# Edge attention in a four-block network: the whole mask on VectorE, finished rows normalised by GpSimd, weighted turned rows written by ScalarE

## The reference, cut to what matters

```python
def edge_score(a):
    s = jnp.einsum('bid,bjd->bij', hidden * a, hidden)
    return jax.nn.leaky_relu(s, 0.2)
alpha = jnp.where(adj == 1, edge_score(a0), NEG_INF)   # a1..a3 for adj == 2, 3, 4
alpha = jax.nn.softmax(alpha, axis=-1)
return jnp.matmul(alpha, hidden)      # x = x + this, hidden = layernorm(x)
```

## Time and profile before

| | us |
|---|---|
| median of 3 runs (lowest, highest) | 1168.76 (1166.08, 1174.06) |
| the profiled execution, its own time | 1170.39 |
| its span, first to last instruction | 1168.6 |
| TensorE busy in it | 1100.7 (94%) |
| VectorE, ScalarE, GpSimd busy in it | 704.9, 744.0, 415.9 |
| edge attention: 64 steps, from first to last L2031 | 301.7 |

### The profile page before, as it was taken

One profiled execution on the slowest core, in us unless ns is written; L12 is line 12 of the kernel. 1 busy time (PEld: TensorE's weight loads), 2 busy tenths in 40 slices (PEclk: granted clock), 3 DMA queues, 4 the chain that ended last, 5 costly groups with the idle time before them and its releaser, 6 DMA issues. The chain is left out here.

```text
span 1168.6 us, 18925 instructions
## 1 busy us (share of the span) xinstructions
PE 1100.7 (94%) x5993; PEld 725.8 (62%) x5993; DVE 704.9 (60%) x2210; ACT 744.0 (64%) x1074; POOL 415.9 (36%) x475
## 2 busy tenths in 40 slices
PE   2998899899999999689999999998999999999998
PEld 2554445444477777557777777776546666666667
DVE  4779888888663436287888888864443333333335
ACT  2887777788665554366777777775666556565561
POOL 5327677866765222344556565211000000000000
PEclk9999899899999999899999999999999999999999
DMA  8977557655227665412222222110000000000001
GB/s 260 343 292 265 183 214 285 254 207 210 75 89 245 186 195 168 131 44 84 84 82 82 80 84 80 56 54 1 1 1 10 19 10 10 19 10 19 10 10 37
DMA packets 69142, 131.08 MB, mean 112 GB/s; under 512 B 9918, under 2 KB 30764, under 8 KB 68012
## 3 DMA queue, kind: packets, MB, share of 16 engines
q1 hardware_dynamic: 60268, 111.96, 28.5%
q0 software_dynamic: 8192, 16.79, 4.7%
q10 hardware_dynamic: 576, 1.05, 0.3%
HBM read 77.60 MB, written 52.17 MB: 111 GB/s over the span
## 5 line engine op out<-in xcount | busy, mean ns | idle before, releaser
L2227 PEld LDWEIGHTS eY<-Vo,dGW 128*128 128x128 f32 x1024 | 132.4, 191 | 54.0 <-issue 52.8
L507 POOL DMA_INDIRECT sorted_x<-V,AT_I x128 | 125.9, 984 | 55.8 <-issue 36.2
L2210 PE MATMUL eU<-XTN,V 128*128 128x512 f32 x256 | 132.9, 602 | 2.5 <-PEq L2145 2.5
L2227 PE MATMUL eY<-Vo,dGW 128*128 128x128 f32 x1024 | 134.2, 276 | 0.1
L673 PE MATMUL O<-Y,HS 128*128 128x512 f32 x256 | 134.0, 644 | 0.0
L1863 POOL DMA_INDIRECT W<-sorted_y,ROW_I x96 | 101.0, 1052 | 90.5 <-PE f_T L1923 71.7
L2218 PE MATMUL eU<-H,V 128*128 128x512 f32 x256 | 131.4, 595 | 0.0
L2397 DVE TENSOR_TENSOR dGW<-H,WBC 128x512 f32<-128x512 f32 x80 | 55.2, 691 | 125.2 <-PE eY L2227 125.0
L1942 PEld LDWEIGHTS f_O<-f_XN,f_PT 128*128 128x128 f32 x896 | 107.8, 192 | 25.3 <-issue 20.7
L2306 ACT ACTIVATE H<-eU,bn 128x512 f32<-128x512 f32 x128 | 99.5, 777 | 30.4 <-PE eU L2210 21.3
L1995 ACT COPY f_PT<-f_TP 128x512 f32<-128x512 f32 x128 | 68.7, 589 | 73.2 <-PE f_TP L1932 73.2
(11 more groups left out here) (305 smaller groups left out, 2034.2 us busy)
## 6 DMA issues: line engine op xcount, KB each, us to landing
XTN<-in_adj SPq DMA_DIRECT2D x64, 512.0 KB, 4.7
masks<-NMW SPq DMA_DIRECT2D x8, 2048.0 KB
f_MK<-masks SPq DMA_DIRECT2D x60, 256.0 KB, 2.7
sorted_y<-zero SPq DMA_DIRECT2D x39, 256.0 KB, 10.1
NMW<-sorted_x SPq DMA_DIRECT2D x39, 256.0 KB, 2.7
sorted_y<-NMW SPq DMA_DIRECT2D x39, 256.0 KB, 2.5
X<-in_x SPq DMA_DIRECT2D x8, 512.0 KB, 7.7
out_x<-X SPq DMA_DIRECT2D x16, 256.0 KB, 2.3
```

Source lines behind the costliest of these rows:

```text
L507: g_.indirect_dma_start(sorted_x, bass.IndirectOffsetOnAxis(ap=AT_I[b % 2][:, kt:kt + 1], axis=0), XR[b % 2][:, t * P:(t + 1) * P], None). ...
L2210: pe.matmul(U1[j % 2][:, :], V1[:, e * P:(e + 1) * P], XTN[:, b * N + q * HALF:b * N + (q + 1) * HALF], start=True, stop=True).then_inc(u1 ...
L2227: i = pe.matmul(Y[q][:, t * P:(t + 1) * P], GW[:, j % 2, t * P:(t + 1) * P], Vo[:, e * P:(e + 1) * P], start=(e == 0 and t == 0), stop=(e ...
```

## The change

Three pieces of work move to another engine, and one to another form. VectorE adds the mask to all 1024 columns of `R4`; TensorE's identity matmul with the mask, and its wait for the mask load, go. GpSimd does `norm_next`, straight after `root_next` in r = 4, with the negated means in the new tile `LESS`. ScalarE writes `XTA` from `M` with the scale `a0`, just ahead of its copy of `M` into `XT`, and `weigh` goes from VectorE. In r = 0 of a batch TensorE also waits until the second half of `XT` is copied.

```diff
+                def norm_next(b):                        # GpSimd
+                    if b >= 1:
+                        pool.wait_ge(m_ps, nth["n", b - 1, 1] + 1)
+                    nc.gpsimd.tensor_scalar(LESS[:, :], MVN[:, b % 2, :, 0], -1.0, 0.0, ALU.mult, ALU.add).then_inc(pstep, 1)
+                    pool.wait_ge(pstep, step.next())
+                    pool.wait_ge(next_rs_ready, b + 1)
+                    for t in range(NT):
+                        i = nc.gpsimd.tensor_scalar(XNN[:, t * P:(t + 1) * P], X[:, (b * NT + t) * P:(b * NT + t + 1) * P],
+                                                    LESS[:, t:t + 1], RSN[:, 1, t:t + 1], ALU.add, ALU.mult)
+                    i.then_inc(next_xn_ready, 1)
...
                         if r == 4 and b > 0:
                             root_next(b - 1)
+                            norm_next(b - 1)
...
                     if r == 0 and b >= 1:                # TensorE, scores(g)
                         pe.wait_ge(xta_ready, 2 * b)
+                        pe.wait_ge(m_read, nth["x", b, 1] + 1)
                     if g >= 2:
                         pe.wait_ge(y_ready, g - 1)
-                    pe.matmul(T[g % 2][:, 0:HALF], xta(b)[:, r * P:(r + 1) * P], xt(b)[:, 0:HALF], start=True, stop=False)
-                    if g == 0:
-                        pe.wait_ge(late_loaded, 16 * E // 2 * (len(late_loads) + 1))
-                    if g >= RING:
-                        pe.wait_ge(loaded[g % RING], 16 * (g // RING))
-                    pe.matmul(T[g % 2][:, 0:HALF], identb[:, :], mask(g)[:, 0:HALF], start=False, stop=True)
-                    pe.matmul(T[g % 2][:, HALF:N], xta(b)[:, r * P:(r + 1) * P], xt(b)[:, HALF:N], start=True, stop=True
-                              ).then_inc(t_ready, 1)
+                    for h in range(2):
+                        i = pe.matmul(T[g % 2][:, h * HALF:(h + 1) * HALF], xta(b)[:, r * P:(r + 1) * P],
+                                      xt(b)[:, h * HALF:(h + 1) * HALF], start=True, stop=True)
+                    i.then_inc(t_ready, 1)
...
                         if b >= 3:                       # ScalarE, copy_turned, kind "x"
                             act.wait_ge(t_ready, (b - 1) * NT)
-                            act.wait_ge(xta_ready, 2 * b - 4)
+                        nc.scalar.activation(XTA[:, b % 2, h * HALF:(h + 1) * HALF], M[:, :], ACT.Copy, scale=a0
+                                             ).then_inc(xta_ready, 1)
                     nc.scalar.copy(dst, M[:, :]).then_inc(m_read, 1)
...
-                    v.tensor_tensor(R4[:, g % 2, HALF:N], R4[:, g % 2, HALF:N], mask(g)[:, HALF:N], ALU.add).then_inc(barred, 1)
+                    v.tensor_tensor(R4[:, g % 2, :], R4[:, g % 2, :], mask(g), ALU.add).then_inc(barred, 1)
...
-                def norm_next(b):                        # VectorE
-                def weigh(b):                            # VectorE
```

More of the change, by code:

```diff
@@ L1786, in one_kind @@
             STN, MVN, RSN = tile("STN", [P, NT, 6]), tile("MVN", [P, 2, NT, 2]), tile("RSN", [P, 2, NT])
+            LESS = tile("LESS", [P, NT])
             YG = [w[:, :].rearrange("p (k d) -> p k d", d=P) for w in (W1, W2)]
@@ L2052, in mean_next @@
                         i.then_inc(next_mv_ready, 1)
-                def norm_next(b):
-                    if b >= 1:
-                        dve.wait_ge(m_ps, nth["n", b - 1, 1] + 1)
-                    ln_apply(dve, b, MVN[:, b % 2, :, :], RSN[:, 1, :], XNN, 0, next_rs_ready, next_xn_ready)
                 def join(b, tiles):
@@ L2093, in norm @@
                     i.then_inc(xn_ready, 1)
-                def weigh(b):
[L2096 to L2101, removed]
                 joins, joined_at = Count(), {}
@@ L2111, in prepare @@
                             norm(1)
-                        if r == 7:
-                            weigh(1)
                     elif b < LAST:
@@ L2119, in prepare @@
                             norm(b + 1)
-                        if r == 6:
-                            weigh(b + 1)
                     if b + 2 < B and r == 7:
@@ L2133, in _ @@
                     prepare(g // NT, g % NT)
-                    if g >= NT and g % NT == (6 if g < LAST * NT else 5):
-                        norm_next(g // NT - 1)
                 for g in range(G - 3, G):
```

## The result

| | before | after |
|---|---|---|
| median of 20 runs, us | 1171.85 | 1176.79 |
| the profiled execution, its own time / span | 1170.39 / 1168.6 | 1177.56 / 1175.8 |
| first to last reduction, us | 301.73 | 308.27 |

The ratio is 1.0046, with a 95% interval from 1.0024 to 1.0067: half a per cent slower. Of the 7.2 us by which the profiled span grew, 6.5 lie in the 64 steps of the stage. The first reduction starts 1.2 us later and 0.6 us less follows behind the last.

The account below looks back on a forecast made before the run. TensorE, at 4.60 us a plain step, led a circle of 4.25; lengthened to 4.78, the circle would bind. 301.1 + 2.7 + 2.9 + 1.7, less 0.7, against 301.7: 6.0 us slower, about 1174.8 us, range 1163 to 1188.

Parts of the forecast that it names:

- 63 steps at the circle's 4.78: All intervals from first to last reduction, each at the lengthened lap: 301.1 us, against 301.7 before.
- the circle: Closed lap of ScalarE and VectorE: rectifier, mask addition, reduction, exp, next rectifier; 4.25 us before, 4.78 with 0.53 added.
- seven steps with `norm`, +0.39 each: One step per batch where VectorE still normalises before its reduction stays 0.39 us above the circle: 2.7 us.
- steps with `feature`: GpSimd's sum of features holds up VectorE's joins: 0.5 us in three steps, 1.35 in batch 6, together 2.9 us.
- mask additions held off by `norm_next`: VectorE's mask additions wait for one of GpSimd's eight normalisations at most: 0.25 us a batch, 1.7 us in all.
- first tile and first laps: First tile's scores ready earlier without the mask matmul, first laps of batch 0 slightly under 4.25: 0.7 us off.
- the lower of the two bounds: VectorE's mask addition on 1024 columns: 1.22 us, like the reduction, against at most 1.38, two of the present instruction.
- The rival that TensorE stays the bound: Stage stays bound by TensorE, the circle has unseen slack, and 13.4 us come out: 1155 us; chance 0.05.
- ScalarE's second write: Writing `XTA` from `M`, about 0.6 us, two per batch: just fits before the exp, costed at nothing; uncovered, 4 us.
- The upper bound: In r = 5 or 6, each collision of normalisations and mask addition costs up to a whole GpSimd instruction: 0.61 twice a batch.
- the second rival: GpSimd's eight normalisations hold off a mask addition for their whole run, up to 4.3 us a batch: about 1204; chance 0.07.
- the delay that `norm_next` and `weigh` caused in r = 6: About 3 us on VectorE after a reduction, about 2.4 free: some 0.5 us delay before the change, worth nothing further.

Follow-up runs that it names:

- mask_only: Kernel before, with VectorE adding the mask to all 1024 columns and TensorE's mask matmul gone; norm_next and weigh stay on VectorE: 1186.77 us, ratio 1.0108.
- no_mask: Changed kernel with VectorE's mask addition left out, so no mask at all: 1154.48 us, ratio 0.9818 to the kernel before.
- relu_first: Changed kernel with ScalarE's relu(g) put before prob(g - 1) in each step: 1170.16 us, ratio 0.9982 to the kernel before.
- feature_later: Changed kernel with GpSimd's feature moved from r = 1 to r = 4, behind norm_next: 1186.43 us, ratio 1.0146 to the kernel before.
- feature_gated: Changed kernel with feature moved to r = 3, released by the end of that step's mask addition: 1171.34 us, ratio 0.9983 to the kernel before.
- both: Changed kernel with relu(g) before prob(g - 1) and feature moved to r = 4, behind norm_next: 1164.18 us, ratio 0.9910 to the kernel before.
- both_gated: Changed kernel with relu(g) before prob(g - 1) and feature in r = 3, released by that step's mask addition: 1157.52 us, ratio 0.9872 to the kernel before.

## Why the prediction was right

Forecast were 1174.8 us, a ratio of 1.0052; measured are 1176.79 us and 1.0046. In the stage the profiled executions lie 6.5 us apart where 6.0 were forecast, and the medians of all runs 4.9. By its terms, in us of the stage:

| term | forecast | measured |
|---|---|---|
| 63 steps at the circle's 4.78 | 301.1 | 301.1 |
| seven steps with `norm`, +0.39 each | 2.7 | 2.7 |
| steps with `feature` | 2.9 | 4.6 |
| mask additions held off by `norm_next` | 1.7 | 0.0 |
| first tile and first laps | -0.7 | -0.2 |
| sum | 307.7 | 308.2 |

The mask addition on 1024 columns takes 1.22 us, the lower of the two bounds and the value taken. The circle did decide. mask_only lengthens it, and takes work from TensorE, and its plain steps grow to 4.78. no_mask and relu_first change nothing but the circle of the changed kernel; the mean step of batch 1, 4.83 in the changed kernel, is 4.54 and 4.65 in them. The rival that TensorE stays the bound fell with mask_only.

Two terms were mis-sized, by the same 1.7 us in opposite directions. That they cancel is luck; it brought the sum within 0.6 us of the measured one. The feature steps are 5.90, 5.91, 5.89 and 6.04 us long; this is the first of the four, to be set against the earlier trace rows:

```profile
658.98 1.96 POOL L1864 DMA_INDIRECT W<-sorted_y,ROW_I  x1 [0.31 <-issue]
...
660.14 1.23 DVE L2042 CUSTOM_DVE_ANT_0 f_Y<-f_T,f_R 128x1024 f32<-128x1024 f32 x1
...
660.97 2.36 POOL L1892 TENSOR_TENSOR FT<-FT,XTN 128x1024 f32<-128x1024 f32 x1
...
662.03 2.31 DVE L2075 SCALAR_TENSOR_TENSOR X<-W,SHARE,X 128x128 f32<-128x128 f32 x4
...
666.05 1.22 DVE L2042 CUSTOM_DVE_ANT_0 f_Y<-f_T,f_R 128x1024 f32<-128x1024 f32 x1
```

I had `feature` start 0.1 us before the reduction. It starts 0.83 after it, just as before, since the second gather ahead of it takes 1.96 us: it began 0.1 us after the mask addition and could end only behind it. So the joins wait their full 1.2 us. I had priced that wait for VectorE only; GpSimd pays too.

The other term, with ScalarE's second write, is in the steps of r = 5 and 6:

```profile
679.52 1.22 DVE L2038 TENSOR_TENSOR f_R<-f_R,f_MK 128x1024 f32<-128x1024 f32 x1
...
679.93 0.87 POOL L1877 TENSOR_SCALAR f_LESS<-f_MVN 128x8 f32<-128x8 f32 x1
...
680.84 0.70 ACT L1984 ACTIVATE f_XTA<-f_M,pcol 128x512 f32<-128x512 f32 x1
680.90 3.47 POOL L1881 TENSOR_SCALAR b<-X,f_LESS,f_RSN 128x128 f32<-128x128 f32 x8
...
681.42 0.60 ACT L1986 COPY f_XT<-f_M 128x512 f32<-128x512 f32 x1
...
682.05 1.15 ACT L1998 ACTIVATE f_Y<-f_Y,f_LOW 128x1024 f32<-128x1024 f32 x1
...
683.20 1.00 ACT L1992 ACTIVATE f_R<-f_T 128x1024 f32<-128x1024 f32 x1
...
684.30 1.22 DVE L2038 TENSOR_TENSOR f_R<-f_R,f_MK 128x1024 f32<-128x1024 f32 x1 [1.55 <-ACT f_R L1992]
```

GpSimd's first small instruction waited out the mask addition (0.87 us, where it took 0.19 when no addition was under way, in relu_first), and then the eight ran back to back in 3.47 us, 0.43 each and not the 0.61 of the earlier trace rows. They end within 0.1 us of the moment when the next mask addition falls due, and that starts 1.10 us after the rectifier, without a wait. By the rule of the Trainium skill, "SBUF — State Buffer", section "SBUF: two separate sides", the loser of the shared ports waits for the whole instruction of the other. The waits of both engines here agree with it: 1.2 us for the joins, about 1.0 for the gather, 2.2 in feature_later. It isn't borne out where a mask addition starts while a gather is under way: there neither waits (see the last section). The upper bound that I built on it did not come, because the eight and a mask addition hardly met in the changed kernel.

What a real meeting costs stands in relu_first, where a mask addition falls due in the midst of the eight in five of seven batches:

```profile
713.10 4.43 POOL L1881 TENSOR_SCALAR b<-X,f_LESS,f_RSN 128x128 f32<-128x128 f32 x8
714.05 1.43 DVE L2038 TENSOR_TENSOR f_R<-f_R,f_MK 128x1024 f32<-128x1024 f32 x1 [1.04 <-ACT f_R L1992]
```

The addition takes 0.2 us more than its 1.22, less than one of the eight, and the eight take about 1 us more. That is close to the 0.25 us a batch that I had taken for a meeting, and it answers the second rival too: VectorE gets in between two of GpSimd's instructions and doesn't wait for all eight. The size was sound; wrong was that the two would meet.

ScalarE's writes end at 682.02 and the exp that needs ScalarE starts at 682.05, which is 1.27 after the reduction, when it was due. The cover held with nothing left; the scaled write took 691 ns and I had taken 0.6.

The prediction also put the delay that `norm_next` and `weigh` caused in r = 6 at some 0.5 us. In mask_only they made that step 1.2 us longer than the circle. The sum didn't use this figure, since both were gone from VectorE.

## What to carry to other kernels

When one engine shows 98% busy, look for the shortest lap of the others before taking work from it: here 4.60 us stood against a closed circle of 4.25, so 0.21 us saved on TensorE couldn't pay for 0.53 us put into the circle. Look next at which order closes the circle; to exchange two ScalarE instructions, with no work changed, took 5.3 us off the stage of the changed kernel. With the sum of features moved as well, the whole mask on VectorE was worth 5 us where it had cost time before. And release a long GpSimd instruction by the end of the VectorE instruction that it would hold off, instead of leaving it to where the queue happens to stand.

## What the runs showed of the hardware

- A GpSimd gather's issue waits for VectorE's addition of two SBUF tensors: 0.95 us alone, 1.8 to 2.1 with the addition under way, 23 times in the stage of the changed kernel. The other way round no wait shows: eight mask additions of that kernel started while a gather was under way and kept their 1.20 to 1.23 us.
- A rest of TensorE does not always cost it the clock. In feature_later it fell behind two rests of 2.28 us and stayed at 1.00 behind two others of the same length, and in the changed kernel behind one of 2.58 us in batch 0. In feature_gated it was 0.67 in the window in which a rest of 1.84 us ended. What made the difference was left open. In relu_first, both, feature_later and feature_gated each of these falls made one step 0.9 to 1.6 us longer than the same step elsewhere.
- Most of the scatter between runs comes from the stages before this one. In the twelve profiled executions the first reduction starts at 493.6 to 507.1 us, while from the last reduction to the end it takes 365.9 to 371.4. The windows of the first 330 us, of feature_gated and of both_gated, show granted shares of 0.96 and 0.91 for the same code:

```profile
0.00:330.00 330.00, 286.10 (x1474) 155.02 (x1475) 260.41 (x973) 242.90 (x340) 209.91 (x278) 0.96 0.66 232
...
0.00:330.00 330.00, 286.87 (x1414) 150.87 (x1415) 251.87 (x933) 235.29 (x325) 202.42 (x267) 0.91 0.65 229
```

The profiled execution of both_gated reaches its first reduction at 505.8 us and that of feature_gated at 494.8. A ratio of a few runs carries these 11 us; within the stage the changed kernel's plain steps repeat to 0.01 us from batch to batch. That also bounds what is claimed here: feature_gated is 2.8 us longer than before in the stage, while its ratio of 0.9983 doesn't tell it from no change. Why the clock of the first stage differs from run to run wasn't tried.
